# One-hots of a graph kernel's first aggregation, made tile by tile

## The reference, cut to what matters

```
msgs = edge_vals[:, None] * x[edge_src]
agg = jax.ops.segment_sum(msgs, edge_dst, num_segments=N)
...
deg = jnp.maximum(jax.ops.segment_sum(jnp.ones(dst.shape, jnp.float32), dst, num_segments=6250), 1.0)
deg_isqrt = deg ** (-0.5)
xn = _layernorm(x, axis=-1)
x = x + _L0_gnn_ref(xn, src, dst, edge_weight, deg_isqrt[:, None], ...) + _L0_mix_ref(xn[None], ...)[0]
```

## Time and profile before

| | |
|---|---|
| median of 3 runs | 3971.13 us (3969.26 to 3977.46) |
| the profiled execution's own time | 3973.01 us |
| its span | 3971.2 us |
| busy: TensorE matmul, GpSimd, VectorE, ScalarE | 2855.2, 2553.1, 1763.2, 781.5 us |
| granted TensorE clock, mean | 0.881 |
| first aggregation | about 164 to 1207 us of the span |

### The profile page before, as it was taken

The page is one execution under the profiler, slowest core; times in us unless marked ns, Lnnn a source line. Parts: engine busy times, 40 slices in busy tenths (PEclk is TensorE's granted clock), DMA queues, the critical chain, the costliest instruction groups (busy, mean ns, idle before and its releaser), DMA issues. The chain is left out here.

```text
span 3971.2 us, 42640 instructions
## 1 busy us (share of the span) xinstructions
PE 2855.2 (72%) x13014; PEld 2164.6 (55%) x13014; DVE 1763.2 (44%) x4542; ACT 781.5 (20%) x1777; POOL 2553.1 (64%) x2689
## 2 busy tenths in 40 slices
PE   6767767777767747787777766665577777777878
PEld 5555555555554435575555545444455565666647
DVE  6544444444443752353333333222355555555533
ACT  2211111111112313331111101001122222222220
POOL 3477777777770252447777777776777777777701
PEclk9888888888888879898999988887899999999869
DMA  3343444444433356774444433333444444444405
GB/s 110 95 121 115 120 120 115 120 121 119 117 116 88 119 161 204 222 220 118 125 125 125 119 111 112 111 111 95 119 127 130 130 128 126 130 130 130 127 27 195
DMA packets 281073, 501.73 MB, mean 126 GB/s; under 512 B 61307, under 2 KB 181505, under 8 KB 280698
## 3 DMA queue, kind: packets, MB, share of 16 engines
q0 software_dynamic: 126240, 345.85, 30.2%
q1 hardware_dynamic: 137452, 139.10, 11.3%
q10 hardware_dynamic: 17136, 13.84, 1.1%
HBM read 412.72 MB, written 85.58 MB: 125 GB/s over the span
## 5 line engine op out<-in xcount | busy, mean ns | idle before, releaser
L1308 PE MATMUL bank<-g,m 128*128 128x256 f32 (+1 forms) x4704 | 1542.8, 454 | 882.6 <-DMA g<-d_t,src_i 555.3
L1231 POOL DMA_INDIRECT g<-d_t,src_i x1568 | 1508.2, 962 | 513.9 <-issue 513.9
L1308 PEld LDWEIGHTS bank<-g,m 128*128 128x128 f32 x4704 | 915.1, 221 | 1198.8 <-issue 401.7
L1231 POOL DMA_INDIRECT g<-d_xn,src_i x784 | 795.3, 1014 | 254.9 <-issue 254.9
L1256 DVE TENSOR_SCALAR m<-iota,rel_f,ew_f 128x128 f32<-128x128 f32 x1568 | 420.6, 361 | 326.8 <-PE bank L1308 321.3
L1272 DVE TENSOR_TENSOR accT<-bank,accT 128x256 f32 x294 | 122.7, 417 | 666.9 <-PE bank L1296 666.6
L1237 ACT ACTIVATE s<-bank 128x256 f32<-128x256 f32 (+1 forms) x294 | 111.6, 380 | 921.5 <-PE bank L1308 464.8
L1259 DVE TENSOR_TENSOR eq<-iota,rel_f 128x1024 bf16<-128x1024 f32 x98 | 119.9, 1223 | 48.2 <-PE bank L1310 47.8
L1310 PE MATMUL bank<-ones_b,eq 128*128 128x1 bf16 x784 | 139.3, 178 | 0.0
L219 POOL TENSOR_TENSOR rsd<-ved,mhalf 128x2 f32<-128x2 f32 (+1 forms) x25 | 18.9, 757 | 180.7 <-DVE ved L213 180.5
L1172 PE MATMUL bank<-wg,side_lg 128*128 128x256 f32 (+1 forms) x392 | 130.1, 423 | 2.9 <-DVE side_lg L1164 2.9
(11 more groups left out here) (388 smaller groups left out, 4285.5 us busy)
## 6 DMA issues: line engine op xcount, KB each, us to landing
g<-d_t,src_i POOLq DMA_INDIRECT x1568, 2.7
g<-d_xn,src_i POOLq DMA_INDIRECT x784, 2.8
side_xn<-d_xn SPq DMA_DIRECT2D x96, 128.0 KB, 2.5
d_x<-x SPq DMA_DIRECT2D x48, 256.0 KB, 3.7
d_swT<-wkv SPq DMA_DIRECT2D x48, 256.0 KB, 3.5
swT<-d_swT SPq DMA_DIRECT2D x24, 512.0 KB, 3.3
xt<-d_xs POOLq DMA_DIRECT2D x80, 128.0 KB, 2.8
d_ys<-y ACTq DMA_DIRECT2D x80, 128.0 KB, 2.4
```

Source lines behind the costliest of these rows:

```text
L1231: pool.indirect_dma_start(g[n % RING][:, u, 0:D], None, table, bass.IndirectOffsetOnAxis(ap=k.src_i[:, t:t + 1], axis=0)).then_inc(gathere ...
L1308: ins = pe.matmul(b[:, 0:GW], m[o][:, u, :], g[r][:, u, :], start=(u == 0), stop=(u == GT - 1 and not count))
```

## The change

In the first aggregation, `prepare` made the one-hots of a group with two TENSOR_TENSOR over all eight tiles, the first with broadcast operands, the second with eq as its input. It now makes them with two TENSOR_SCALAR a tile, sixteen a group, whose destination and weight are scalars per partition. The weighted one is computed from iota again and no longer from eq. The values in m and eq, their types and buffers are as before. The wait on `eq_done` is gone.

```
-                dve.tensor_tensor(eq[r][:], k.iota[:].rearrange("p (a n) -> p a n", a=1).to_broadcast([P, GT, P]),
-                                  k.rel_f[:, e].rearrange("p (u a) -> p u a", a=1).to_broadcast([P, GT, P]), ALU.is_equal).then_inc(eq_done, 1)
-                wait(dve, eq_done, n + 1)
-                dve.tensor_tensor(m[r][:], eq[r][:], k.ew_f[:, e].rearrange("p (u a) -> p u a", a=1).to_broadcast([P, GT, P]), ALU.mult).then_inc(m_done, 1)
+                for u in range(GT):
+                    t = n * GT + u
+                    dve.tensor_scalar(eq[r][:, u, :], k.iota[:], k.rel_f[:, t:t + 1], None, ALU.is_equal)
+                    ins = dve.tensor_scalar(m[r][:, u, :], k.iota[:], k.rel_f[:, t:t + 1], k.ew_f[:, t:t + 1], ALU.is_equal, ALU.mult)
+                ins.then_inc(m_done, 1)
```

## The result

The changed kernel takes 3931.19 us in the median of four runs (3925.75 to 3936.93), the kernel before 3971.89 (3969.26 to 3977.46): a ratio of 0.9896, with a 95% interval from 0.9875 to 0.9917. Forecast were 3927, in a range from 3917 to 3945. The profiled execution took 3936.93 us, the longest of the four.

The account below looks back on a forecast made before the run. GpSimd's indirect gathers were taken to bound the first aggregation. Of 51.3 us excess, 0.7 stays and 5.6 of new stalls come, so 45 are won: 3973.0 becomes 3928.0, median 3926, given as 3927; range 3917 to 3945.

Parts of the forecast that it names:

- GpSimd's gathers set the pace of the stage: First aggregation: 784 indirect gathers of L1231, issued one behind the other by GpSimd, set the time; they take 1035 us.
- "no change" rival: First aggregation: gathered rows arrive no sooner despite faster issue, or TensorE sets the pace; 3971 us, chance 0.04.
- A gather stands to the end of L1259, less 0.13: First aggregation: gathers overlapping the long VectorE instruction L1259 last until about its end; 99 gathers lose 50.6 us together.
- 5.6 + 0.7 us come in its place: First aggregation, of 51.3 us excess: 5.6 us of stalls from short TENSOR_SCALAR, 0.7 us that never belonged to L1259.
- The stage's 45 us: First aggregation: predicted gain, the gathers' 51.3 us of excess less 0.7 and 5.6.
- small-gain rival: First aggregation: sixteen short instructions cost more than twice eight, leaving 34.6 us excess; 16 won, 3955 us, chance 0.06.
- VectorE's added work is covered: First aggregation: 110 to 200 us more VectorE work costs nothing, absorbed by its idle waits before L1270 and L685.
- The eq kind passes elements at the double rate, m need not: One-hot instructions: one-scalar TENSOR_SCALAR takes 0.52 ns an element; the two-scalar m kind might not run that fast.
- The slower rival, eq holds GpSimd off: First aggregation: gathers stand while eight eq instructions run, 1.56 us a group, 153 us in all; 4073 us, chance 0.05.
- The last step of the sum, from 3926 to 3927: Whole time: profiled 3973.0 becomes 3928.0, the runs' median is 1.9 lower, so 3926, which the prediction rounded to 3927.

Follow-up runs that it names:

- e12: Changed kernel with the edge-counting matmul for only the first tile of a group (wrong degrees), relieving TensorE; 3929.53 us, ratio 0.9887 to the kernel before.
- e7: The changed kernel unaltered, run again beside the kernel before in a long session (B); ratio 1.0011.
- e8: The changed kernel unaltered, run once more beside the kernel before in another long session (C); ratio 1.0021.
- e2: Kernel before with only eq made by eight short TENSOR_SCALAR a group, m still one TENSOR_TENSOR of 128x1024; ratio 0.9953 to the kernel before, long session.
- e3: Changed kernel plus one unused TENSOR_SCALAR of 128x1024 with one scalar a group; 4466.1 us in a single execution of a long session, no ratio.
- e4: Changed kernel plus one unused TENSOR_SCALAR of 128x1024 with two scalars a group; 4403.2 us in a single execution of a long session, no ratio.
- e1: Kernel before with its two long TENSOR_TENSOR cut into sixteen of 128x128 a group; ratio 0.9999 to the kernel before, long session.

## Why the prediction was right

- *GpSimd's gathers set the pace of the stage.* Right for the result: the gathers' busy time fell by 43.5 us and so did the stage. e12 shows it from the other side. It isn't a property of the kernel alone, though. What my "no change" rival forecast, with 4% of the chance, e7 and e8 measured in sessions in which the kernel before takes 12 to 13% longer. There GpSimd waits for TensorE's products; whether TensorE's own work set the pace, as the rival had it, no run shows, since e12 met the other kind of session. The prediction set no condition on the session, so that the result came from one of the shorter kind was luck.
- *A gather stands to the end of L1259, less 0.13.* Right, and e2, e3 and e4 repeat it with other instructions (1.08 left, 0.94 lost; 0.53 left, 0.39 lost). The count was a little off: 8 of the 99 gathers had started before L1259 did, lost 1.4 us together to the end of L702, and only overlap L1259; the other 91 lost 49.2. That L1262 escaped only by phase was read from two timeline rows and is shown by e2. The law is that of the long instructions. Of the 120 gathers in the changed kernel that meet a short TENSOR_SCALAR with more than 0.25 us of it left, 118 lose nothing (at most 0.02), where it would have them lose 0.12 or more.
- *5.6 + 0.7 us come in its place.* 7.8 came; in other executions of the same kernel 4.8 and 4.0. The stage's 45 us were 43.5. The small-gain rival, 34.6, is far off.
- *VectorE's added work is covered.* Sixteen took 3.74 us of the 3.6 to 4.5, 602.7 us busy in the stage of the 590 to 680. The waits ahead of L1270 (now L1271) shrank from 184.4 to 105.5 us and ahead of L685 from 190.2 to 153.1: that is where the work went. GpSimd never had to wait.
- *The eq kind passes elements at the double rate, m need not.* Wrong in its second half: with two scalars, 1024 elements take 800 ns. It changed nothing, as the price had come from L1256 itself.
- *The slower rival, eq holds GpSimd off,* had the right mechanism and the wrong size. It does hold it, and so does m, but only to the end of one short instruction. The 1.56 us a group would have needed a chain of stalls. The prediction had no row of one; e1 has them, up to 0.77 us, for short TENSOR_TENSOR. With those in place of TENSOR_SCALAR the rival would have been nearer, though at 17 to 19 us still far from 153.
- *The sum, against the whole.* The span fell by 36.1 us, the median by 40.7, the stage by 43.5. The prediction carried the stage's gain over to the whole one for one. In the profile 6.3 us are given back between the first aggregation's last gather and the second's first (576.3 us before, 582.6 after). TensorE's granted clock (the last figure but two) in part of that stretch, before, changed and in e12:

```profile
1340.00:1476.00 136.00, 72.33 (x478) 63.66 (x476) 96.87 (x366) 34.90 (x67) 71.69 (x82) 0.75 0.51 160
```

```profile
1300.00:1436.00 136.00, 74.33 (x471) 65.58 (x469) 95.54 (x360) 33.38 (x64) 70.72 (x81) 0.70 0.50 158
```

```profile
1295.00:1431.00 136.00, 73.12 (x461) 64.37 (x459) 95.39 (x364) 33.23 (x64) 70.58 (x81) 0.70 0.49 156
```

It is 0.70 after and 0.75 before, with almost the same busy time of the engines. An accident of the slowest of four executions it hardly is: e12, another kernel with the same sixteen instructions in another session, has 581.5 us and 0.70 there too. As the kernel before has one profile only, whether the edit brings this with it stays open. The last step of the sum, from 3926 to 3927, is no rounding, and changes nothing.

## What to carry to other kernels

Where GpSimd's issue of indirect gathers is the pace, look for gathers above their median and for what VectorE runs beside them. A long instruction with two tensors from SBUF, or a long TENSOR_SCALAR at the double rate, held the gather until it ended; sixteen short TENSOR_SCALAR with more work in sum were better than two long instructions (7.8 us of excess against 51.3), and sixteen short TENSOR_TENSOR lay between (17.0 and 19.1). A TENSOR_REDUCE of 1.21 us and a RECIPROCAL of 1.75 us, each with one operand in SBUF, did no harm. And see first who waits for whom: where GpSimd waited for TensorE's products, shorter gathers gained nothing (1.0011 and 1.0021).

## What was not expected of the hardware

The same program took 3973 and 4454 us on the same chip in two sessions, and 4447 to 4488 on three chips, with the mean granted clock of TensorE at 0.80 against 0.88 and pauses of TensorE, for most of which the profile names no cause. A TENSOR_REDUCE of 1.21 us didn't lengthen a single one of 97 gathers, a TENSOR_SCALAR of 0.80 us lengthened all that had more than 0.14 us of it ahead. Inside the long instructions the losses follow one line, time left less 0.13 or 0.14 us, for TENSOR_TENSOR and TENSOR_SCALAR alike; short TENSOR_TENSOR in a row held a gather for up to 0.77 us, short TENSOR_SCALAR in a row for no more than 0.20, in all runs of the changed kernel.
